# Decoder layers on one core: exponentials times group probabilities for four heads in one VectorE instruction, with a newly searched order

## The reference, cut to what matters

```python
    def _L1_xattn_ref(query, key_in, value, group_prob, mask, ...):
        q = _split_heads(query @ wq_k + wq_b, H)          # H = 16 heads of 16 columns
        ...
        logits = jnp.einsum('bhqd,bhkd->bhqk', q, k) / jnp.sqrt(...)
        neg = (1.0 - mask.astype(q.dtype)) * -1000000000.0
        logits = logits + neg[:, None, :, :]
        attn = jax.nn.softmax(logits, axis=-1)
        attn = attn * group_prob[:, None, :, :]
        out = jnp.einsum('bhqk,bhkd->bhqd', attn, v)
```

## Time and profile before

| | |
|---|---|
| median of 3 runs | 1528.74 us (1528.48 to 1529.73) |
| the profiled execution: its own time | 1530.75 us |
| its span, from the first to the last instruction | 1528.9 us |
| granted TensorE clock, mean | 0.970 |
| busy: PE, DVE, ACT, POOL | 1394.6, 1067.5, 792.8, 145.4 us |

### The profile page before, as it was taken

The page is one execution under the profiler, slowest core; times in us unless marked ns, Lnnn a source line. Parts: engine busy times, 40 slices in busy tenths (PEclk is TensorE's granted clock), DMA queues, the critical chain, the costliest instruction groups (busy, mean ns, idle before and its releaser), DMA issues.

```text
span 1528.9 us, 29464 instructions
## 1 busy us (share of the span) xinstructions
PE 1394.6 (91%) x9607; PEld 785.1 (51%) x9607; DVE 1067.5 (70%) x2424; ACT 792.8 (52%) x1512; POOL 145.4 (10%) x166
## 2 busy tenths in 40 slices
PE   6788899999999999999999999999999988897990
PEld 3456576564463544343343533434555545796990
DVE  4886744467664787799999999997878774331315
ACT  5465755446558576645465455545666535232330
POOL 1001010100100100010010000000000030023204
PEclk8899999999999999999999999999999999998996
DMA  6223322421412322232312322012322236975753
GB/s 225 77 72 102 103 52 74 114 69 50 127 37 78 109 55 61 61 90 77 90 62 78 97 74 78 19 41 52 94 60 52 55 97 194 318 233 174 224 183 117
DMA packets 119392, 153.78 MB, mean 101 GB/s; under 512 B 31756, under 2 KB 99724, under 8 KB 117260
## 3 DMA queue, kind: packets, MB, share of 16 engines
q1 hardware_dynamic: 116178, 143.51, 31.8%
q0 software_dynamic: 3072, 8.39, 1.7%
HBM read 72.93 MB, written 18.35 MB: 60 GB/s over the span
## 4 chain that ended last, share of the span: by engine, by line
PE 63%; DVE 12%; issue 10%; DMA 5%; SPq 4%; ACT 4%; POOL 1%; DVEq 0%; POOLq 0%; ACTq 0%
PE ps L1210 20%; PE ps L1405 8%; PE ps L1440 6%; PE ps L1371 4%; PE ps L1304 4%; DVE ps L1923 3%; PE ps L1365 3%; PE ps L1362 3%; PE ps L1431 3%; PE ps L1435 2%; PE ps L1404 2%; DMA sorted<-room_h,place 2%; SPq L1112 2%; DVE room_h L1954 1%; SPq L1143 1%
## 5 line engine op out<-in xcount | busy, mean ns | idle before, releaser
L1632 ACT ACTIVATE prob<-ps 128x512 f32<-128x512 f32 (+3 forms) x832 | 404.7, 550 | 210.4 <-PE ps L1405 115.8
L1927 DVE TENSOR_REDUCE mx<-ps 128x1 f32<-128x512 f32 (+3 forms) x512 | 281.2, 585 | 73.2 <-PE ps L1373 37.7
L1405 PE MATMUL ps<-of_expert 99*128 99x512 bf16 (+4 forms) x768 | 251.8, 355 | 6.1 <-DMA of_expert<-mrow 2.4
L1405 PEld LDWEIGHTS ps<-of_expert 99*128 99x128 bf16 (+1 forms) x768 | 73.3, 97 | 95.8 <-ACT prob L1632 35.0
L2099 DVE SCALAR_TENSOR_TENSOR room_b<-room_b,ps 128x512 f32<-128x512 f32 x46 | 31.6, 687 | 125.7 <-ACT room_b L1667 109.0
L1440 PE MATMUL ps<-prob,va 128*32 128x512 f32 (+3 forms) x1024 | 116.4, 529 | 0.7 <-ACT prob L1632 0.4
L1371 PE MATMUL ps<-of_expert 120*128 120x512 bf16 x256 | 91.8, 380 | 4.9 <-issue 1.6
L1365 PE MATMUL ps<-of_expert 96*128 96x512 bf16 x256 | 87.1, 381 | 8.3 <-DVE mx L1923 7.1
L1923 DVE CUSTOM_DVE_ANT_0 ps<-ps,room_a 128x512 f32<-128x512 f32 x128 | 86.1, 709 | 4.9 <-PE ps L1365 4.5
L1923 DVE CUSTOM_DVE_ANT_0 ps<-ps,room_b 128x512 f32<-128x512 f32 x128 | 86.0, 709 | 1.0 <-PE ps L1365 0.9
L1954 DVE TENSOR_TENSOR room_h<-prob,room_b 128x1024 f32<-128x1024 f32 x64 | 78.0, 1244 | 1.0 <-ACT prob L1632 1.0
(11 more groups left out here) (222 smaller groups left out, 2604.2 us busy)
## 6 DMA issues: line engine op xcount, KB each, us to landing
of_expert<-parts SPq DMA_DIRECT2D x384, 128.0 KB, 2.4
room_a<-in_w SPq DMA_DIRECT2D x38, 512.0 KB, 4.8
room_b<-in_w SPq DMA_DIRECT2D x18, 512.0 KB, 4.5
otc<-oraw SPq DMA_DIRECT2D x256, 32.0 KB, 2.0
sorted<-y SPq DMA_DIRECT2D x2, 2944.0 KB, 11.7
ct<-in_c SPq DMA_DIRECT2D x8, 512.0 KB, 3.6
of_expert<-in_w SPq DMA_DIRECT2D x8, 512.0 KB, 6.5
wa<-in_attention SPq DMA_DIRECT2D x4, 768.0 KB, 4.9
```

Of the source, the lines that this page charges most:

```text
L1405: i = pe.matmul(dst[:, lo:S], ks[0:rows, h, t], qs[0:rows, h, lo:S], start=(a != MASKED), stop=(a != CAUSAL and not fixed))
L1632: act.activation(prob[:, quad % PROBS, n, lo:S], key_bank(*st)[:, lo:S], ACT.Exp).then_inc(s_exp, 1)
L1927: i = dve.tensor_reduce(mx[:, slot, s, n:n + 1], src[:, 0:width], AX.X, ALU.max)
```

## The change

Step E becomes one for a quad: it waits for the fourth head's exponential (before, the first half waited for the second head's) and multiplies four heads, 2048 elements a partition, in one instruction (L1953 of the new program). V waits for it. In parts_of it is reckoned at 2.2 us in place of twice 1.15. The table LAG has new numbers, found by a search, so the steps of the whole program are in a new order; two lines of each table stand below. Nothing else is computed differently.

```diff
                 if a == MASKED:
-                    grouped += [("E", u, g, s, 0), ("E", u, g, s, 1)]
+                    grouped += [("E", u, g, s)]
...
-        u, g, s, h = rest
+        u, g, s = rest
...
-        return [("DVE", 1.15, [(("T", u, g, s, 2 * h + 1), "ACT")] + more)]
+        return [("DVE", 2.2, [(("T", u, g, s, J - 1), "ACT")] + more)]
...
-            more += [(("E", u, g, s, 1), "DVE")]
+            more += [(("E", u, g, s), "DVE")]
...
-LAG = {"IN": -7.5, "CA": 11.2, ("CA", 0): -1.5, ("CA", 1): 17.1, "FS": -0.2, "FZ": 28.1, "SO": -1.1, "OP": -4.8, ("OP", 0): 1.6,
-       ("OP", 1): -4.4, ("OP", 2): -26.5, ("OP", 3): -12.2, "M": -0.3, ("M", 1): 0.4, ("M", 2): -0.9, "C": -7.4, ("C", 0): -12.4,
...
+LAG = {"IN": -9.3, "CA": 11.2, ("CA", 0): -1.4, ("CA", 1): 16.2, "FZ": 28.0, "SO": 10.7, "OP": -4.8, ("OP", 0): 1.0, ("OP", 1):
+       -4.4, ("OP", 2): -12.5, ("OP", 3): -7.9, "M": -0.3, ("M", 1): 0.4, "C": -5.8, ("C", 0): -13.4, ("V", 1): 0.2, ("C", 1):
...
-                        pe.wait_ge(s_e, nth("E", u, g, s, 1))
+                        pe.wait_ge(s_e, nth("E", u, g, s))
...
-                    dve.wait_ge(s_exp, nth("T", u, g, s, 2 * h + 1))
-                    two = slice(2 * h, 2 * h + 2)
-                    dve.tensor_tensor(weighed[:, quad % GROUPED, two, :], prob[:, quad % PROBS, two, :],
-                                      masks(seq_of(u))[2][:, s:s + 1, :].to_broadcast([P, 2, S]), ALU.mult).then_inc(s_e, 1)
+                    dve.wait_ge(s_exp, nth("T", u, g, s, J - 1))
+                    dve.tensor_tensor(weighed[:, quad % GROUPED, :, :], prob[:, quad % PROBS, :, :],
+                                      masks(seq_of(u))[2][:, s:s + 1, :].to_broadcast([P, J, S]), ALU.mult).then_inc(s_e, 1)
```

More of the change, by code:

```diff
@@ L1944, in _ @@
                 elif kind == "E":
-                    u, g, s, h = st[1:]
+                    u, g, s = st[1:]
                     quad = QUAD_AT["V", u, g, s]
```

## The result

The change made the kernel slower. Its median over seven runs is 1539.73 us (1534.63 to 1545.22) beside 1528.48 us (1524.60 to 1529.81) for before on the same chip; the ratio is 1.0085, 95% interval 1.0059 to 1.0111, so the loss is 11 us by the medians and 13 us by the ratio. The forecast was 1523.9 us; the time lies above its range, on the other side. The profiled execution took 1534.63 us, the fastest of the seven, with a span of 1532.8 us; it is only 3.9 us longer than the profiled one of before, so the two profiles show less of the loss than the medians do.

What follows compares the result with a forecast made beforehand. DVE was taken to bound the third attention, PE second. Terms -4.8 - 3.6 + 5.6 - 2.0 = -4.8 us took the median from 1528.74 to 1523.9 us; range 1518.3 to 1533.0.

Steps and rivals of the forecast that it cites:

- Part 1 (-4.8): DVE products in the third attention: 128 become 64, each holding DVE 2.195 us against 2.27 a pair; -4.8 us.
- Part 2 (nothing): Product waits for all four exponentials; weighed values take 2.2 us, not 1.1, PE waiting for V's second half; costed at nothing.
- The cover: For the later product: three exponential buffers, and two scores ready in the score banks, 1.26 us of work for DVE.
- Part 3, the add (-3.6): Units 8 and 9: GpSimd's bias add would meet score maxima, no longer a DVE product; 1.8 us each time, -3.6 us.
- second rival: "The gain is eaten": GpSimd's add meets a product again, +3.6, time 1527.5 us; no change 0.27, with weaker mixtures.
- Part 3, runs of scores (+5.6): Third attention: 48 additional maxima third or later in a run wait for PE's refill; +5.6 us, 0.2 each behind a V.
- Part 3, projections (-2.0): DVE's four stops for ScalarE's first part, 3.9 us: projections partly strewn between products, half the stops go; -2.0 us.
- The slower one: Rival: DVE runs short of scores at the 8 maxima behind a V; runs cost 16.6, time 1534.9 us; chance 0.22.
- The check "DVE waits for scores more than 8 us": Sign that the forecast is wrong, in the third attention's stretch; the other was time outside it moving over 3 us.

Runs made afterwards that it cites:

- e18: Before, with GpSimd's bias add of units 10 and 11 waiting until the product it used to meet is done: 0.9975 of before, stage 387.6 us.
- e1: Order of before kept step for step, only the two products of a quad merged into one at the second's place: 1.0035 of before, stage 397.6 us.
- e17: Order of before, products left as two of two heads, both issued late and waiting for the fourth exponential: 1.0038 of before, stage 400.0 us.
- e9 to e11: After, before, and before's order with merged products, each without fillers between first and last E: 1.0146, 1.0030 and 1.0059 of before.
- e2: Order of after, each product issued as two of two heads, the first waiting for the second head's exponential: 1.0081 of before, stage 407.8 us.
- e3: Before's order with merged products, QK of units 10 and 11 moved to where after has them: 1.0186 of before, stage 421.6 us.
- e14: As e3, plus another buffer so ScalarE's copy for odd units need not wait for the DMA: 1.0099 of before, stage 405.2 us.
- e13: After, plus a second buffer so ScalarE's copy for odd units need not wait for the DMA: 1.0081 of before, stage 405.7 us.
- e4: After, with three QK projection steps of units 10 and 11 moved back by one or two quads: 1.0113 of before, stage 411.1 us.

## Why the prediction was wrong, point by point

**What bounds the kernel.** The text took DVE for the bound and PE for second. That holds: DVE's stops in the stage before come to 9.1 us of 391.2, and in e18 3.6 us off DVE were 3.6 us off the stage. What does not hold is the condition, "as long as PE keeps it fed", which was taken as met on the strength of the fillers. In e1 and e17 PE stopped at V, DVE's stops grew from 9.1 to 20.0 and 17.8 us, and the stage by 6.4 and 8.8. The rows in hand could have warned of it: in the earlier trace rows the products follow each other from 814.80 to 817.62 without a wait of their own. Fillers in the stage as a whole say nothing of such a stretch, and e9 to e11 show that they can't be given up.

**Part 1 (-4.8).** The size on DVE was right. After, a product holds DVE from 692.08 to 694.29, 2.21 us, and 2.204 in the median (2.195 forecast):

```profile
692.08 2.29 DVE L1953 TENSOR_TENSOR room_h<-prob,room_a 128x2048 f32<-128x2048 f32 x1 [0.18 <-ACT prob L1632]
694.29 0.69 DVE L1923 CUSTOM_DVE_ANT_0 ps<-ps,room_a 128x512 f32<-128x512 f32 x1
```

What failed is that it counts in full. With nothing but the merge changed, 64 x (2.27 - 2.204) = 4.2 us less on DVE were worth 2.4 us of the stage (e17 to e1), and DVE's stops took up the rest (17.8 to 20.0 us). In the order of after the merge and its later start together are worth 0.9 (e2 to after).

The Trainium skill's "VectorE: DVE Perf Modes" (TRN2 errata) has a fixed 151 cycles in its formula for an fp32 tensor_tensor; by that, 10.1 us would have gone, an estimate. As a duration the formula gives 2291 ns for 2048 elements, which agrees with the bar (2.29 us); but the engine took the next instruction after 2.21 us.

**Part 2 (nothing).** This step failed. The cover that I named, two scores in hand, is DVE's. The wait is PE's: V's second half stands at the head of PE's queue, and scores stand behind it, the very scores of the cover. e17 prices it at 8.8 us of the stage in the order of before. The remark that PE's wait for products "may grow without harm" was wrong there: 5.0 to 28.5 us in e1. In the order of after that wait is only 6.3 us; that the search bought this with its other losses is not shown.

**Part 3, the add (-3.6).** e18 confirms the price, 3.6 us. In the new order only one of the two went: the add of unit 10 now meets the projection's third part, which lasted 2.79 us where the others take 1.22.

```profile
703.68 2.79 DVE L1900 TENSOR_TENSOR parts<-rest,parts 128x1024 bf16<-128x1024 f32 x1
...
706.39 0.69 DVE L1923 CUSTOM_DVE_ANT_0 ps<-ps,room_a 128x512 f32<-128x512 f32 x1
```

```profile
703.39 2.00 POOL L1752 TENSOR_TENSOR x<-x,pack 128x1024 f32<-128x1024 f32 x1 [11.41 <-PE ps L1215]
```

So 1.6 of the 3.6 us came back. The text had named that danger, the projections' third part too, as its second rival.

**Part 3, runs of scores (+5.6).** DVE's waits for scores of this attention rose by 4.7 us (1.9 to 6.6), and by 7.8 with the 3.1 for those of the next. The sign was right and the sum near, but by luck: runs without a V kept 0.62 to 0.70 us in all but one place, and six maxima behind a V came 1.12 to 1.75 us after the one before them, 0.5 to 1.1 over 0.66 where 0.2 was reckoned.

**Part 3, projections (-2.0).** By DVE's stops this is the step that weighs most in the kernel after, and its sign was wrong: DVE's waits there went from 5.3 to 17.0 us. I read from the order that projections were strewn between products, and did not ask when `parts` comes free. SP issues the DMA that empties it just ahead of them in the new order. When a step is moved, every queue that it is moved past has to be read, SP's too. e3 and e14 show the price of that place in the order of before; in the order of after, halving the wait won 1 us at most (e13, e4), so how much of the loss goes through it there is open.

**The sum.** The order was to cost -3.6 + 5.6 - 2.0 = 0; alone it costs 16.6 us of the stage (e2). DVE's waits in the stage rose by 11.7 us for projections, 7.8 for scores and 1.9 for weights of the next attention (L1819), and fell by 1.1 for exponentials; the add gave 2.0 and the merge 4.2 us of its time. That is 20.3 - 6.2 = 14.1 us, measured 15.7. This says where DVE stood, and not what each cause is worth: e13 takes 4.7 of the 11.7 us away, and the stage gets 1.2 us shorter. What is shown is that the order as a whole is the loss, in stops of DVE for projections and scores, that the additional fillers are not behind it, and that halving the wait for the DMA does not bring it back. Which places of it would have to change is open.

**The rivals.** The slower one had the mechanism half right, DVE out of scores, and reckoned 1534.9. But the maxima behind a V stayed under the 1.2 us over 0.66 from which it was to decide, and the projections, the larger share, stood in no rival. The check "DVE waits for scores more than 8 us" came true at 9.7, though 3.1 of that belong to the next attention. Outside the stage the time moved by more than 3 us as well, but that bound was badly chosen, as the last section shows.

## What to carry to other kernels

When an instruction on the busiest engine is merged, its result comes later by the first half's time; price that on the engine that consumes it, at the head of that engine's queue, before counting what the merge saves. Where two engines are both nearly full, time taken off one is worth only what the other can follow: 4.2 us less on DVE gave 2.4. A table that a search found for one set of steps is to be measured again when a step changes. Look first for collisions of two engines at one place: one wait on GpSimd gave 3.6 us, and 64 merged products gave nothing.

## What the runs showed of the hardware that I had not expected

GpSimd's add delays a DVE product of two SBUF operands until it ends, whatever the product's size: 1.8 us for one of 1024 elements (3.02 against 1.22) and 1.8 for one of 2048 (4.09 against 2.29). The Trainium skill's "SBUF — State Buffer" (two separate sides) calls it an exclusive lock held for the whole instruction; by that the product of the earlier trace rows starts at 675.54 + 2.19 = 677.73 and its bar ends 1.22 later, at 678.95. The row has 675.79 + 3.02 = 678.81, so the trace agrees to 0.14 us.

The first 650 us differ between executions with the same instructions (the chip may be another one as well). e17 has the program of before up to the third attention, yet its copy of unit 7 came at

```profile
646.21 0.60 ACT L1642 ACTIVATE oraw<-ps 128x512 f32<-128x512 f32 x1 [1.13 <-PE ps L1441]
```

6.8 us ahead of before. In the window from 160 to 210 us the clock was 0.97 of full in before and 1.00 in e17:

```profile
160.00:210.00 50.00, 46.31 (x377) 31.84 (x377) 29.51 (x69) 33.56 (x51) 2.95 (x6) 0.97 0.36 97
```

```profile
160.00:210.00 50.00, 46.42 (x420) 33.43 (x420) 28.82 (x69) 32.60 (x51) 2.95 (x6) 1.00 0.37 99
```

So the difference of one profile against another outside the place of a change is no evidence below 7 us here. Inside the stage, with both ends taken in the same execution, one pair shows how steady the length is: e18 and before differ there by two waits of GpSimd alone. The ends of e18's stage:

```profile
650.40 0.60 ACT L1641 ACTIVATE oraw<-ps 128x512 f32<-128x512 f32 x1 [1.14 <-PE ps L1440]
...
1038.03 0.60 ACT L1641 ACTIVATE oraw<-ps 128x512 f32<-128x512 f32 x1 [1.23 <-PE ps L1435]
```

Counted from the stage's start, its copies are 1.8 us ahead of those of before after the first wait and, from the second on, 3.59 to 3.61 us ahead at each of the twelve copies that are left. So differences of the stage as small as those between e17, e1 and e2 can be read, though each kernel was profiled once.
